# A stacked 64-row MLP chunk, rotation ahead of the final addition, and three attention mixes in a row

## The reference

```
mods = silu(c) @ adaln_w + adaln_b          # shift, scale, gate for both halves
x_mod = rms(x) * (1 + scale_msa) + shift_msa
q, k, v = split(x_mod @ qkv_w)              # 16 heads of 16
q, k = rope(rms(q, lnq_w), rms(k, lnk_w))
x = x + gate_msa * (softmax(q k^T / 4) v @ proj_w + proj_b)
h = rms(x) * (1 + scale_mlp) + shift_mlp
x = x + gate_mlp * ((silu(h @ w1_w) * (h @ w3_w)) @ w2_w)     # hidden width 704
self = concat(x, cond) @ W_self.T + b_self  # cond is zero where a row of x sums to 0
for d in 0, 1:                              # two directions of the edges
    w = softmax(q_d k_d^T / 4, masked by the edges, + edge bias)    # 16 heads, 20 keys
    out += (w @ self[:, :20]) @ Wout_d + bout_d
y = x + relu(self + out)
```

## Time and profile before

| | |
|---|---|
| runs | 1388.95 us median of 3 (1387.53 to 1390.21) |
| profiled execution | 1389.65 us, its span 1387.1 us |
| PE busy | 1322.3 us, 95% |
| PE weight load busy | 1227.1 us, 88% |
| DVE busy | 1184.9 us, 85% |
| ACT busy | 888.7 us, 64% |
| POOL busy | 716.9 us, 52% |
| mean granted TensorE clock | 0.98, full between 100 and 1300 us |

### The profile page before, as it was taken

The page is one execution under the profiler, slowest core; times in us unless marked ns, Lnnn a source line. Parts: engine busy times, 40 slices in busy tenths (PEclk is TensorE's granted clock), DMA queues, the critical chain, the costliest instruction groups (busy, mean ns, idle before and its releaser), DMA issues.

```text
span 1387.1 us, 51521 instructions
## 1 busy us (share of the span) xinstructions
PE 1322.3 (95%) x20276; PEld 1227.1 (88%) x20276; DVE 1184.9 (85%) x2065; ACT 888.7 (64%) x1784; POOL 716.9 (52%) x676
## 2 busy tenths in 40 slices
PE   4579999999999999999999999999999999999985
PEld 4478999999999999999999999999999999999985
DVE  5667998898889889888988998898899889889763
ACT  4546666667666666766666676666667666666542
POOL 0235555545655554565555456555545655554442
PEclk9789999999999999999999999999999999999997
DMA  7001111001111100111110011111000111100100
GB/s 245 30 24 31 46 44 44 20 31 35 43 43 43 43 21 31 35 43 43 43 43 23 31 32 43 43 43 43 24 31 32 43 43 43 43 28 24 31 22 9
DMA packets 49827, 56.19 MB, mean 41 GB/s; under 512 B 4352, under 2 KB 47744, under 8 KB 49792
## 3 DMA queue, kind: packets, MB, share of 16 engines
q1 hardware_dynamic: 48944, 53.86, 12.1%
q10 hardware_dynamic: 848, 1.84, 0.4%
HBM read 47.03 MB, written 8.65 MB: 40 GB/s over the span
## 4 chain that ended last, share of the span: by engine, by line
PE 90%; issue 1%; DVE 1%; ACT 0%; POOL 0%; ACTq 0%; DVEq 0%
PE psum L486 51%; PE psum L622 5%; PE psum L728 4%; PE psum L758 4%; PE psum L792 4%; PE psum L607 4%; PE psum L775 3%; PE psum L806 3%; PE psum L587 2%; PE psum L696 2%; PE psum L570 2%; PE psum L631 1%; PE psum L534 1%; PE psum L526 1%; PE psum L541 0%
## 5 line engine op out<-in xcount | busy, mean ns | idle before, releaser
L1318 POOL TENSOR_TENSOR gl<-gf,gh 128x512 fp32r<-128x512 f32 x96 | 124.5, 1297 | 254.2 <-ACT gh L926 254.2
L486 PE MATMUL psum<-nh,w_lo 128*128 128x256 f32 x704 | 182.4, 290 | 0.1
L486 PE MATMUL psum<-nh,w_hi 128*128 128x256 f32 x704 | 176.7, 281 | 0.0
L1318 POOL TENSOR_TENSOR nl<-xn,nh 128x512 fp32r<-128x512 f32 x64 | 100.3, 1568 | 124.4 <-ACT nh L864 124.4
L486 PEld LDWEIGHTS psum<-nh,w_hi 128*128 128x128 f32 x704 | 133.1, 189 | 0.0
L486 PEld LDWEIGHTS psum<-nh,w_lo 128*128 128x128 f32 x704 | 132.5, 188 | 0.5 <-issue 0.5
L1384 POOL TENSOR_TENSOR e<-e,inv 128x640 f32<-128x640 f32 x64 | 82.0, 1281 | 88.2 <-DVE inv L1274 88.2
L486 PE MATMUL psum<-nl,w_hi 128*128 128x256 f32 x704 | 115.4, 282 | 0.0
L926 ACT ACTIVATE gh<-gf 128x512 fp32r<-128x512 f32 x96 | 60.3, 628 | 61.6 <-DVE gf L1202 60.9
L486 PEld LDWEIGHTS psum<-nl,w_hi 128*128 128x128 f32 x704 | 97.4, 188 | 0.0
L486 PE MATMUL psum<-qkv_lo,nh 128*128 128x512 f32 (+1 forms) x256 | 88.0, 355 | 3.7 <-ACT nh L864 2.8
(11 more groups left out here) (186 smaller groups left out, 4451.5 us busy)
## 6 DMA issues: line engine op xcount, KB each, us to landing
adj<-in_adj SPq DMA_DIRECT2D x32, 440.0 KB, 3.3
x_in<-in_x SPq DMA_DIRECT2D x32, 256.0 KB, 2.6
xn<-in_xT SPq DMA_DIRECT2D x32, 256.0 KB, 3.5
x_res<-in_xT SPq DMA_DIRECT2D x32, 256.0 KB, 3.6
out_T<-y SPq DMA_DIRECT2D x32, 256.0 KB, 2.2
e<-in_adaln ACTq DMA_DIRECT2D x2, 512.0 KB, 5.1
stage<-in_qkv SPq DMA_DIRECT2D x2, 384.0 KB, 4.8
pT<-in_w SPq DMA_DIRECT2D x2, 384.0 KB, 6.2
```

The source lines that it names most:

```text
L486: last = nc.tensor.matmul(out, lhsT, rhs, start=start and i == 0, stop=stop and i == len(terms) - 1)
L1318: return nc.gpsimd.tensor_tensor(out, full, hi.bitcast(F32), ALU.subtract)
```

## The change

- The half chunk's combined product goes to z, next to the full chunk of w1, and its w2 weights stand twice, in rows 0 to 63 and 64 to 127. The high part of the half chunk is copied by a new ACT step `half_high` into rows 0 to 63 of the last chunk of `gl`, whose rows 64 to 127 hold the low part. Four products over 128 rows take the place of six over 64. ACT has one tanh of 128x512 for n = 2, DVE two silu and two products.
- `rope` of both tiles stands behind `rope_scale` and ahead of `out`.
- PE's mix(1), mix1(0) and mix1(1) stand together behind mlp_up(2). mix(1) uses bank 2; the second graph tile has its own `pT` buffer. ACT's copy of the values is a step of its own, `values`; that of tile 1 stands behind the tanh of mlp_up(2), since it overwrites the `vb` that mix(1) of the block before reads.

```diff
-    "mix": (5, 6), ...
+    "mix": (5, 2), ...
 ORDER "PE":
-        (1, "mlp_up", 1), (3, "qkv", 0), (0, "probsT1", 0), (2, "mix", 1), (3, "qkv", 1), (0, "mix1", 0),
-        (0, "probsT1", 1), (1, "mlp_up", 2), (0, "mix1", 1), (1, "mlp_down", 0), (1, "mlp_down", 1), (2, "mixT", 0),
+        (1, "mlp_up", 1), (3, "qkv", 0), (0, "probsT1", 0), (3, "qkv", 1), (0, "probsT1", 1), (1, "mlp_up", 2),
+        (2, "mix", 1), (0, "mix1", 0), (0, "mix1", 1), (1, "mlp_down", 0), (1, "mlp_down", 1), (2, "mixT", 0),
...
-        pT0, pT1 = pT[:, 0, :, :], pT[:, 1, :, :]
+        pT0, pT1 = pT[:, 0, :, :], [pT[:, 1, :, :], sb("pT1_1", [P, NJ, P])[:, :, :]]
...
 PE mlp_down:
+                wait(pe, half_hi, m, 1)
                 for o in both:
-                    for i, (w, a) in enumerate(((wl["w2"], gh), (wh["w2"], gh), (wh["w2"], gl))):
-                        last = nc.tensor.matmul(down_ps[:, o, :], w[half, MC - 1, out_chunks[o]], a[half, MC - 1, :],
-                                                start=False, stop=o == DC - 1 and i == 2, tile_position=(HALF, 0))
+                    last = linear(down_ps[:, o, :], high_terms("w2", out_chunks[o], gl, [MC - 1]), False, o == DC - 1)
...
 ACT:
+            def values(m, t):
+                wait(act, qkv_done, m, t + 1)
+                wait(act, mixed, m, t + 1 - TILES)
...
+            def half_high(m, n):
+                wait(act, g_lo, m, MC // 2)
+                nc.scalar.activation(gl[0:HALF, MC - 1, :], gf[HALF:, 1, :], ACT.Copy).then_inc(half_hi.sem, 1)
...
 DVE mlp_up, n = 2:
+                    nc.vector.scalar_tensor_tensor(gf[HALF:, 1, :], th[0:HALF, 1, :], 1.0, z_ps[n][0:HALF, 1, :],
+                                                   ALU.add, ALU.mult).then_inc(half_silu.sem, 1)
                     nc.vector.scalar_tensor_tensor(gf[:, 0, :], th[:, 0, :], 1.0, z_ps[n][:, 0, :], ALU.add, ALU.mult)
...
+                    wait(dve, half_silu, m, 1)
+                    nc.vector.tensor_tensor(gf[HALF:, 1, :], gf[HALF:, 1, :], z_ps[n][HALF:, 1, :], ALU.mult).then_inc(z_silu.sem, 1)
+                    wait(dve, z_silu, m, n + 1)
+                    wait(dve, z_done, m, 2 * n + 2)
+                    nc.vector.tensor_tensor(gf[:, 0, :], gf[:, 0, :], u_ps[n][:, 0, :], ALU.mult).then_inc(g_done.sem, 1)
```

More of the change, by code:

```diff
@@ L73 @@
     "xT": 6, "qk": (2, 3), "v": (7, 1), "heads": (7, 5), "probsT": (5, 4, 4, 7), "probsT1": (0, 5, 4, 7),
-    "mix": (5, 6), "q1": (4, 6), "score": 0, "score1": 0, "mixT": 6, "proj": 2, "norm1": 7, "up": (6, 4, 6),
+    "mix": (5, 2), "q1": (4, 6), "score": 0, "score1": 0, "mixT": 6, "proj": 2, "norm1": 7, "up": (6, 4, 6),
     "gate": (3, 1, 0), "down": 1, "rowsum": 3, "self": 4, "k1": 5, "v1": 7, "mix1": 5,
@@ L89 @@
     "DVE": [
-        (2, "rope", 0), (2, "rope", 1), (0, "mlp_down", 0), (1, "mixT", 0), (1, "proj", 0), (0, "row_mask", 0),
+        (0, "mlp_down", 0), (1, "mixT", 0), (1, "proj", 0), (0, "row_mask", 0),
         (0, "edge_masks", 0), (2, "score_max", 0), (2, "score", 0), (1, "norm1_squares", 0), (2, "score_max", 1),
@@ L95 @@
         (0, "soft1_inverse", 0), (1, "mlp_up", 0), (0, "score1", 1), (0, "soft1", 1), (0, "soft1_inverse", 1),
-        (1, "mlp_up", 1), (1, "edges", 0), (2, "mix", 1), (3, "qkv", 0), (3, "qkv", 1), (1, "mlp_up", 2), (0, "mix1", 0),
-        (3, "rope_scale", 0), (0, "out", 0),
+        (1, "mlp_up", 1), (1, "edges", 0), (3, "qkv", 0), (3, "qkv", 1), (1, "mlp_up", 2), (2, "mix", 1), (0, "mix1", 0),
+        (3, "rope_scale", 0), (3, "rope", 0), (3, "rope", 1), (0, "out", 0),
     ],
     "Activation": [
-        (2, "rope_scale", 0), (0, "mlp_split", 2), (1, "mixT", 0), (0, "x2_split", 0),
+        (2, "rope_scale", 0), (0, "mlp_split", 2), (0, "half_high", 0), (1, "mixT", 0), (0, "x2_split", 0),
         (2, "heads", 0), (2, "heads", 1), (0, "self", 0), (0, "self_split", 0), (1, "norm1_mean", 0), (0, "keys", 0),
@@ L104 @@
         (2, "probsT", 1), (1, "mlp_up", 0), (1, "mlp_split", 0), (0, "score1", 1), (1, "mlp_up", 1),
-        (0, "probsT1", 0), (3, "qkv", 0), (1, "mlp_split", 1), (3, "qkv", 1), (0, "probsT1", 1), (1, "mlp_up", 2),
+        (0, "probsT1", 0), (3, "qkv", 0), (3, "values", 0), (1, "mlp_split", 1), (0, "probsT1", 1), (3, "qkv", 1),
+        (1, "mlp_up", 2), (3, "values", 1),
     ],
@@ L654, in mlp_up @@
[L654 to L655 removed]
+                    groups = [[(z, 0, "w1", MC - 2, True, False), (z, 1, "w1", MC - 1, False, True)], [(u, 0, "w3", MC - 2, True, True)]]
+                for i, group in enumerate(groups):
+                    if (n, i) == (0, 0):
                         wait_free(pe, m, (normed[0], 2, 1), (q1_kept, -1, 2))
[L657 removed]
+                    elif (n, i) == (0, 1):
@@ L666, in mlp_up @@
                         wait_free(pe, m, (pT1_a, -1, 1), (biased1, -1, 4), (shifted_s, 1, 2))
-                    for c, w, j in chunks[name]:
-                        linear(out[:, c, :], high_terms(w, out_chunks[j], nh[1], both), c == 0, False)
-                    if name == "w1":
+                    for out, c, w, j, start, stop in group:
+                        linear(out[:, c, :], high_terms(w, out_chunks[j], nh[1], both), start, False)
+                    if i == 0:
                         wait(pe, normed_lo[1], m, 1)
-                    for c, w, j in chunks[name]:
-                        last = linear(out[:, c, :], low_terms(w, out_chunks[j], nl[1], both), False, c == chunks[name][-1][0])
+                    for out, c, w, j, start, stop in group:
+                        last = linear(out[:, c, :], low_terms(w, out_chunks[j], nl[1], both), False, stop)
```

70 lines of the change are left out of this document (29 added, 41 removed).

## The result

The changed kernel takes 1406.95 us (median of 4 runs, 1402.84 to 1410.35), before 1388.91 in runs on the same chip; the ratio is 1.012 [1.0099, 1.014]. The forecast was 1389.9 with a range to 1398: wrong, in size and in sign. The profiled execution took 1402.84, its span is 1400.5 us.

A forecast was written before the change was run, and what follows sets the result against it. The chain through POOL's gl and low part of x2 was taken as the bound, not PE; table load -0.19 and new order +0.20, with DVE's own work, gave +0.03 a turn, +0.9 us over 31 turns: 1389.9, range 1377 to 1398.

The forecast's parts named there:

- What bounds the kernel: Turn's end in self_feat: PE waits some 0.1 us for POOL's low part of x2; shortening PE alone gives nothing.
- What PE saves: PE's list: mlp_up(2) starts 2.01 us earlier, mix(1) ends at 627.24, PE has 0.7 us a turn less to do.
- what the value copies do: ACT behind mix(1): four copies take 1.14 us, and the table load starts at 628.40 instead of 628.59.
- What DVE does: DVE from rotation sums to rope: silu again at 628.28, gf done at 629.90, rope ready at 631.71 or 631.83.
- just in time for gh: DVE's fourth gf operation ends at 629.90, before ACT's gh could start at 629.95; gl then ends at 631.94.
- later than gl's end by more than a tenth: Sign of being wrong: rope on DVE stands ready more than a tenth of a us after POOL's gl ends.
- What the new order costs: From gl's end to the gate with rope ahead of y: 1.80 to 1.89 us instead of 1.67; 0.20 later taken.
- DVE becomes the bound: Rival: added DVE work and pauses eat y's 0.9 us reserve; +0.2 us a turn, 6 us, 1395; chance 0.25.

The follow-up runs named there:

- stack_only: The kernel before with only the half chunk stacked and made first, mixes and rope order as before: 1398.08 us.
- rot_only: The kernel before with only the two rope operations put ahead of y on DVE: 1399.79 us.
- no_mix: The changed kernel with the mixes back in their old places; stacked half chunk and ropes ahead of y stay: 1405.29 us.
- no_stack: The changed kernel with the half chunk as before (six products, three gf operations); moved mixes and ropes ahead of y stay: 1404.45 us.
- after_three: The changed kernel with three gf operations instead of four, silu of both chunks in one 128x512 operation: 1395.62 us.
- after_early: The changed kernel with ACT's rounding of MLP pair 1 to its high part moved ahead of the first squares: 1407.9 us.
- mix_only: The kernel before with only the mixes and value copies moved, with their bank, second buffer and waits: 1387.34 us.
- stack_three: The kernel before with the stacked half chunk and three gf operations; mixes, ropes and ACT's split as before: 1388.58 us.
- y_from_x1: The changed kernel with y adding x1 instead of x2, so the gate need not wait for y: 1397.85 us.
- no_rot: The changed kernel with y ahead of the ropes again; stacked half chunk and moved mixes stay: 1394.18 us.
- stack_three_early: The kernel before with stacked half chunk, three gf operations and ACT's early split of pair 1; mixes and ropes as before: 1381.54 us.
- norot_three_early: The changed kernel with y ahead of the ropes again, three gf operations and ACT's early split of pair 1: 1399.74 us.

## Why the prediction was wrong

**What bounds the kernel: right.** The chain over POOL's low part ended the turn before and after, PE's saving gave nothing, and PE's waits grew as it got less to do. stack_only shows it by itself.

**What PE saves and what the value copies do: right.** mix(1) starts 6.10 behind probsT1 (predicted 6.21), the table load 0.25 earlier (0.19). Nothing rests on the difference.

**"What DVE does" is the first step that failed.** It listed the right operations and priced the spaces between them too low. Four gf operations at 0.34 apart were to end at 629.90; they end at 634.12 - 3.87 = 630.25. Beside a 64-row operation the starts are 0.43 to 0.45 apart, in the earlier trace rows too (628.28 to 628.71), where I had taken 0.43 for a wait. The step from the second rotation pair to the first of them is 0.12 longer too, and rope's wait for the reciprocal costs 0.18, where 0 and 0.12 were the bounds. In sum rope stands ready at 636.09 - 3.87 = 632.22 instead of 631.71 to 631.83. The same delay reached gl: "just in time for gh" was wrong, gh waits 0.29 for gf, and gl ends at 632.27 instead of 631.94. So both bounds of the prediction came out about half a us late. Rope was to be "later than gl's end by more than a tenth" as a sign of failure; against the forecast end (631.94) it is 0.28 late, against the measured one it is 0.05 early. That sign did not show, since gl had moved as well; the turn of 41.00 in place of 40.4 did.

**"What the new order costs" is the second.** It took 0.04 to 0.13 for the gate's pause behind y, from two other places. Pauses of that size do occur behind a 128x512 too: in before the product L1202 starts 0.13 after the end of the silu it waits for, so the writer's form is not what made the difference. Timeline of DVE of before:

```profile
615.24 0.69 DVE L1193 SCALAR_TENSOR_TENSOR gf<-th,psum 128x512 f32<-128x512 f32 x1 [0.37 <-ACT th L917]
616.06 0.69 DVE L1202 TENSOR_TENSOR gf<-gf,psum 128x512 f32<-128x512 f32 x1
```

Behind y the pause is 0.23 to 0.24 in all six kernels that show it (after, rot_only, no_mix, no_stack, after_three, after_early), and the order by itself costs 0.33 (rot_only) instead of 0.20.

**The rival came nearest.** "DVE becomes the bound" named the queue, its reserve of 0.9 under gl, and the one-to-one price of each pause, and had a chance of 0.25. Its size was two tenths where it is 0.58. It counted pauses of 0.1. By the rows of both kernels the queue grew by 0.12 + 0.20 + 0.63 + 0.18 + 0.02 and by 0.31 for the gate's wait, 1.46 in all, against a reserve of 0.90 (1.51 from y to the rope under gl, 0.61 without): 0.56. The prediction had the 0.63 right (0.64) and put the others low: 0 for the later start, -0.02 for the four operations, 0 to 0.12 for rope's wait, 0.12 to 0.21 for the gate's. All of them were lengths in one queue, and there errors add up. Yet the queue is the last bound only by 0.10: with gl alone as the bound, as in no_mix, the turn would still have grown by 0.47, from the same two errors (gl's end and the new order).

## What to carry to other kernels

Before moving work onto an engine that looks idle, see whether its idle time is a hold that hides slack: here y's 1.58 us were 0.69 of work and 0.9 of reserve, and each of the three edits uses up some of that reserve. Where several edits fill one queue, sum them at their high prices, and treat an operation that needs the last one's result as longer by the overlap and a pause (0.12 to 0.31 us here, by place). Then work out the next bound as well: an edit that shortens the queue alone gains only the distance to it, here 0.10 (no_mix, after_early). An edit that gains alone can lose in company; the pairs tell it, and two runs that undo one part each show it.

## What the runs showed of the hardware

- Successive DVE operations overlap by about 0.08 us (0.69-long ones start 0.61 apart). Where a 64-row one is among them, starts are 0.42 to 0.46 apart for a length of 0.42, also where its inputs had long been ready (no_stack, 636.76 to 637.18). An 8-row operation (gate, L1215 in before) overlaps its follower as the others do, 637.71 to 638.05, so fewer rows alone do not make the difference; the 64-row ones write rows 64 to 127. Which property of theirs decides was not tried.
- DVE's wait for its own last result costs a pause beyond its end that differs by place: 0.23 to 0.24 for the gate behind y, with the turn's branch between them; 0.13 behind the 128x512 silu in before (615.24 + 0.69 to 616.06) and behind a 64x256 (633.15 + 0.42 to 633.70); 0.04 behind the 128x512 silu in after_three (628.16 + 0.68 to 628.88). What sets it stays open.
- A DVE operation with both inputs in SBUF that comes while POOL works on gl stands still: y (1.42 to 1.58), the ropes (1.51, 1.83 in no_mix, 1.99) and the rotation pair (1.36, 1.81) alike. Beside a POOL operation of 128x2 it does not (x_sq, L1086 in before, 0.41 at 642.76). The Trainium skill (SBUF — State Buffer, SBUF: two separate sides) says that the first to start holds the shared ports for its whole instruction; the pair of 1.81 began 0.10 behind a gl and ended 0.62 behind its end, which agrees but for about 0.13: unheld the pair takes 0.75.
- Single turns near the start, and in some kernels near the end, are up to 5 us longer than the steady ones. In the second turn the traces show two parts of it. PE stands still at the graph layer's scores (`score1`) for nothing that they record: 0 in before, mix_only, rot_only, after and after_three, 0.40 in no_mix, 0.98 in after_early, 1.56 in stack_three and y_from_x1, 1.87 to 2.34 in stack_only, no_stack, no_rot, stack_three_early and norot_three_early. And in four of these last five, all but no_rot, the granted clock falls to half for 3.4 us, between 0.1 us before and 1.4 us after PE goes on:

```profile
165.82 0.60 PE L775 MATMUL psum<-kbd,q1T 32*64 32x40 f32 x25 [1.87 <-issue]
```

```profile
166.00:169.40 3.40, 3.40 (x85) 3.21 (x81) 2.71 (x6) 0.00 (x0) 0.20 (x1) 0.50 0.02 5
122.20:125.60 3.40, 3.40 (x69) 2.94 (x61) 2.67 (x5) 1.03 (x2) 0.00 (x0) 0.50 0.02 5
```

  The PE row and the first window are of stack_only; the second window is of before, whose clock is thus not quite full from 100 us on. The second turn is 40.80 to 41.73 us where PE does not stand still, 41.65 to 43.18 where it does, and 44.02 to 45.39 where the clock falls too. Most of the 4 us in stack_only's and no_stack's times that the steady turn does not explain lies there. after_three, after_early and norot_three_early have such a stop (2.12, 1.92, 2.41) in the last turn but one, of 42.59, 43.88 and 44.02 us. What makes PE stand still, and why the clock fell behind four of these stops and not behind the longest one (2.34), stays open.
